# A new order of masks, projections and GpSimd work in a layer of attention and experts

## The reference

```python
qkv = jnp.einsum('bsm,qhdm->bqhsd', x, W_qkv)            # 16 heads of 64
qk_rot = qk * cos + _rotate_half(qk) * sin               # first 32 dims of q and k
scores = jnp.where(causal, -jnp.inf, Q @ K^T) / sqrt(DK)
out = softmax(scores) @ V ; attention = out @ W_o
probs = softmax(x @ router_w + router_b)                 # 8 experts and a skip
top_v, top_i = jax.lax.top_k(probs, 2)
experts = sum over the two of gate * (gelu(x @ w1[e]) @ w2[e]) + gate[skip] * x
```

## Time and profile before

| | |
|---|---|
| median of 3 runs | 1558.59 us |
| profiled execution | 1554.54 us, its span 1552.7 us |
| mean granted clock of TensorE | 0.947 of full |
| PE / DVE / ACT / POOL busy | 81% / 78% / 73% / 52% of the span |
| instructions | 47377 |

### The profile page before, as it was taken

The page is one execution under the profiler, slowest core; times in us unless marked ns, Lnnn a source line. Parts: engine busy times, 40 slices in busy tenths (PEclk is TensorE's granted clock), DMA queues, the critical chain, the costliest instruction groups (busy, mean ns, idle before and its releaser), DMA issues.

```text
span 1552.7 us, 47377 instructions
## 1 busy us (share of the span) xinstructions
PE 1263.4 (81%) x15156; PEld 982.4 (63%) x15157; DVE 1213.7 (78%) x4592; ACT 1134.4 (73%) x3606; POOL 806.5 (52%) x1324
## 2 busy tenths in 40 slices
PE   2415888888888888887899999788888888888887
PEld 2403666666666666665798988566666666666666
DVE  6788777777778777775677777788888888887885
ACT  6415777777777777776588887777877777777776
POOL 3243666666666666665000000466766766666665
PEclk9757999999999999999899999999999999999999
DMA  9522322222222222224122322333333333333330
GB/s 296 183 52 52 79 73 70 71 69 69 70 71 69 70 71 70 69 71 133 52 84 85 88 83 79 77 77 78 76 79 76 86 91 83 81 90 95 79 76 26
DMA packets 115839, 130.19 MB, mean 84 GB/s; under 512 B 11568, under 2 KB 75312, under 8 KB 115376
## 3 DMA queue, kind: packets, MB, share of 16 engines
q1 hardware_dynamic: 107056, 110.26, 28.2%
q0 software_dynamic: 8576, 17.33, 3.9%
HBM read 28.85 MB, written 31.59 MB: 39 GB/s over the span
## 4 chain that ended last, share of the span: by engine, by line
PE 42%; DVE 26%; issue 8%; DMA 5%; POOL 4%; ACT 2%; DVEq 0%; POOLq 0%; ACTq 0%
PE bank L1118 8%; DVE arena L972 8%; PE bank L1189 7%; PE bank L1119 7%; PE bank L1120 7%; DVE arena L934 5%; DMA stage<-sorted_y_dram,rows_at 4%; PE bank L1225 4%; PE bank L1199 4%; DVE arena L945 3%; DVE o_whole L1005 2%; DVE arena L933 2%; PE bank L1209 2%; PE bank L1226 1%; DVE stage L891 1%
## 5 line engine op out<-in xcount | busy, mean ns | idle before, releaser
L643 ACT ACTIVATE probs<-arena,neg_max 128x128 f32<-128x128 f32 (+1 forms) x1024 | 453.3, 446 | 109.6 <-DVE neg_max L972 102.5
L972 DVE CUSTOM_DVE_ANT_0 arena<-bank,causal 128x128 f32<-128x128 f32 (+1 forms) x1024 | 314.8, 344 | 2.7 <-PE bank L1189 2.7
L1189 PE MATMUL bank<-arena 64*128 64x128 f16 (+1 forms) x3072 | 179.4, 252 | 128.8 <-DVE neg_max L972 128.3
L501 POOL DMA_INDIRECT stage<-sorted_y_dram,rows_at x128 | 126.3, 986 | 260.9 <-DMA sorted_y_dram<-stage 238.4
L1199 PE MATMUL bank<-ident,probs 128*128 128x128 f32 x1536 | 241.9, 274 | 5.7 <-ACT probsT L626 5.5
L1189 PEld LDWEIGHTS bank<-arena 64*128 64x128 f16 x3072 | 102.9, 97 | 182.8 <-DVE neg_max L972 128.5
L1199 PEld LDWEIGHTS bank<-ident,probs 128*128 128x128 f32 x1536 | 183.2, 142 | 35.7 <-issue 6.4
L626 ACT ACTIVATE probsT<-bank 128x384 f32<-128x384 f32 x384 | 185.9, 484 | 19.3 <-PE bank L1199 19.2
L643 ACT ACTIVATION_READ_ACCUMULATOR probs<-arena,neg_max 128x1 f32 x1024 | 195.4, 191 | 0.0
L1225 PE MATMUL bank<-probsT,arena 128*64 128x256 f32 x1024 | 187.6, 425 | 0.9 <-ACT probsT L626 0.9
L1118 PE MATMUL bank<-xnT_lo,wqk_hi 128*128 128x256 f16 x512 | 143.4, 280 | 54.9 <-DVE arena L934 50.8
(11 more groups left out here) (155 smaller groups left out, 3430.0 us busy)
## 6 DMA issues: line engine op xcount, KB each, us to landing
arena<-arena SPq DMA_DIRECT2D x256, 256.0 KB, 4.7
arena<-sorted_x_dram SPq DMA_DIRECT2D x72, 128.0 KB, 2.1
sorted_y_dram<-stage SPq DMA_DIRECT2D x72, 128.0 KB, 1.8
sorted_x_dram<-arena SPq DMA_DIRECT2D x3, 2304.0 KB, 16.7
arena<-experts_dram SPq DMA_DIRECT2D x8, 512.0 KB, 5.1
out_dram<-acc SPq DMA_DIRECT2D x32, 128.0 KB
sorted_x_dram<-arena SPq DMA_DIRECT2D x1, 2368.0 KB, 16.2
sorted_x_dram<-stage,rows_at POOLq DMA_INDIRECT x128, 2.3
```

What stands on the lines that cost most here:

```text
L501: nc.gpsimd.indirect_dma_start(out=stage[:, k % BACKS, :], out_offset=None, in_=sorted_y[0:ROWS, :], in_offset=bass.IndirectOffsetOnAxis(a ...
L643: last = nc.scalar.activation(probs[:, s % 4, at:at + w], masked[:, s % 4, at:at + w], ACT.Exp, bias=neg_max[:, s % 4, t:t + 1], scale=-1. ...
L972: last = nc.vector.tensor_tensor_reduce(out=masked[:, s % 4, at:at + w], in0=SC[s % 2][:, at:at + w], in1=causal[:, at:at + w], scale=1.0, ...
L1189: last = mm(SC[h][:, at:at + w], q_stack[parity][rows, r, ql, u, qs], k_stack[parity][rows, r, kl, u, 0:w], start=(n == 0), stop=(n == 2))
```

## The change

1. `mask(b, s)` becomes `masks(b, s)` at even s: both heads of a pair are masked one after the other, then everything else of the two steps follows. A wait for the exps of three heads earlier is added, since the masks run further ahead in their four buffers.
2. The units are placed anew: nine in steps 0 to 11 and five in steps 10 to 15, no longer eight projections in steps 0 to 7. Three of the eight projections of sample b + 2 (plain 0, rotary 0, plain 1) are made in sample b, at steps 10, 12 and 14. Samples 0 and 16 have a denser list (`OPENERS`).
3. ACT's `rope_high` moves from lag 2 to lag 3. The low parts of rotary queries (j = 0 and 1) move from DVE (lag 3) to GpSimd (lag 4); those of keys stay.
4. The rows to send are normalised on GpSimd, just ahead of their send, and the slots are read in place, without `rows_at`. GpSimd's waits for indirect DMAs stand right before what needs them; `pause` is gone. One gather moves from step 9 to 10.
5. Inverses are taken for four heads at once, at steps 0, 4, 8 and 12, behind that step's evictions, scaling and unit work; the splits follow directly.
6. In DVE's order `o_scale` stands before the unit work.

```diff
-BESIDE = [
-    [("rest", 0)], [("rope", 0)], [("rest", 1)], [("rope", 1)],
-    [("rest", 2)], [("rope", 2)], [("rest", 3)], [("rope", 3)],
-    [("v_high", 0)], [], [("v_high", 1)], [("y", 0)],
-    [("y", 1)], [("v_low", 0)], [("v_low", 1)], [],
-]
+OPENERS = ((0, "rest", 0), (1, "rope", 0), (2, "rest", 1), (3, "rope", 1), (4, "rest", 2), (6, "rope", 2),
+           (7, "v_high", 0), (8, "rest", 3), (9, "v_high", 1), (10, "rope", 3))
+USUAL = ((0, "rope", 1), (2, "rest", 2), (4, "rope", 2), (5, "v_high", 0), (6, "rest", 3), (7, "v_high", 1),
+         (8, "rope", 3), (9, "y", 0), (11, "y", 1))
+AHEAD = ((10, "rest", 0), (12, "rope", 0), (14, "rest", 1))
+VALUES = ((13, "v_low", 0), (15, "v_low", 1))
-GATHER_AT = [1, 3, 5, 7, 9, 9, 11, 13]
+GATHER_AT = [1, 3, 5, 7, 9, 10, 11, 13]
...
 def o_split(J, j, parity):
     pool.wait_ge(o_scaled, J + 1)
-    nc.gpsimd.tensor_tensor(pause[:], half[:, 0:1], half[:, 0:1], ALU.add)
...
+def q_rope_low(j, m):
+    pool.wait_ge(rope_hi, ROPES * m + j + 1)
+    hi, lo = parts("rope", j)
+    nc.gpsimd.tensor_tensor(lo, roped[j % 2], hi, ALU.subtract).then_inc(q_rope_lo, 1)
+
+def normalise_row(b, i):
+    tile = PER * b + i
+    pool.wait_ge(sent, 16 * TOP * tile)
+    nc.gpsimd.tensor_scalar(stage[:, i, :], acc[:, tile, :], neg_mean[:, tile:tile + 1], rstd[:, tile:tile + 1],
+                            ALU.add, ALU.mult).then_inc(send_ready, 1)
...
+# GpSimd, step s: o_split; rope_add of the unit at s - 1; q_rope_low of the rotary unit at s - 4 (j < 2);
+# then normalise_row (even k) and send, or gather
...
-for kind, j, u, psum, n in beside(b, at, s - 2):
+for kind, j, of, u, psum in due(b, s, 3):
     if kind == "rope":
-        rope_high(j, b + 1)
+        rope_high(j, of)
...
+def masks(b, s):
+    dve.wait_ge(s_ready, 8 * b + s // 2 + 1)
+    if not (b == 0 and s < 4):
+        dve.wait_ge(exp_done, 16 * b + s - 2)
+    for i in range(2):
+        for t, (at, w) in enumerate(((0, P), (P, 2 * P))):
+            last = nc.vector.tensor_tensor_reduce(out=masked[:, (s + i) % 4, at:at + w], ...)
+        last.then_inc(s_masked, 1)
+
+def invert(N, n):
+    dve.wait_ge(exp_done, QUAD * N + QUAD)
+    nc.vector.reciprocal(inv, total[:, of, :]).then_inc(inv_done, 1)
+    if N >= 2:
+        dve.wait_ge(inv_turned, 2 * N - 2)
+    dve.wait_ge(inv_done, N + 1)
+    nc.vector.tensor_scalar(hi, inv, W_SCALE, None, ALU.mult).then_inc(inv_hi, 1)
+    dve.wait_ge(inv_hi, N + 1)
+    nc.vector.scalar_tensor_tensor(lo, inv, W_SCALE, hi, ALU.mult, ALU.subtract).then_inc(inv_ready, 1)
...
+def beside(b, s, at):       # DVE: t_evict, o_scale, turn / rest_low / y_add of the unit at s - 1,
+                            # invert at s % 4 == 0, rope_low of a key unit at s - 3, mix at s == 0, combine
+def sample(b, parity, at):
+    for s in range(0, H, 2):
+        masks(b, s)
+        beside(b, s, at)
+        beside(b, s + 1, at)
```

More of the change, by code:

```diff
@@ L505, in sample @@
+            pool.wait_ge(routed, 1)
+            pool.wait_ge(cleared, 16 * 5)
             def sample(b, parity, at):
                 for s in range(H):
[L507 to L520, removed]
                     if not (at in FILLS and s < SPLIT_LAG) and (s - SPLIT_LAG) % 2 == 1:
                         o_split(8 * b + (s - SPLIT_LAG - 1) // 2, (s - SPLIT_LAG) % H // 2, parity if s >= SPLIT_LAG else 1 - parity)
-                    for kind, j, u, psum, n in beside(b, at, s - 1):
+                    for kind, j, of, u, psum in due(b, s, 1):
@@ L524, in sample @@
                         if kind == "rope":
[L525 to L529, removed]
+                            rope_add(j, of)
+                    for kind, j, of, u, psum in due(b, s, 4):
+                        if kind == "rope" and j < 2:
+                            q_rope_low(j, of)
+                    if b < MID and s in SEND_AT:
+                        k = SEND_AT.index(s)
+                        if k % TOP == 0:
+                            normalise_row(b, k // TOP)
+                        send(b, k)
@@ L531, in rest_of @@
+                    if b >= MID and s in GATHER_AT:
+                        gather(b, GATHER_AT.index(s))
             def rest_of(b):
@@ L917, in mix @@
             def mix(b):
+                if b < MID:
+                    dve.wait_ge(send_ready, TPS * b + TPS)
                 for t in range(TPS):
@@ L962, in _ @@
             router_mix()
-            def mask(b, s, at_fill):
-                if s % 2 == 0:
-                    dve.wait_ge(s_ready, 8 * b + s // 2 + 1)
-                    if not (at_fill and s < INV_LAG):
-                        invert(8 * b + (s - INV_LAG) // 2, (s - INV_LAG) % H // 2)
-                for t, (at, w) in enumerate(((0, P), (P, 2 * P))):
-                    last = nc.vector.tensor_tensor_reduce(
-                        out=masked[:, s % 4, at:at + w], in0=SC[s % 2][:, at:at + w], in1=causal[:, at:at + w],
-                        scale=1.0, scalar=MASKED, op0=ALU.add, op1=ALU.min, accum_out=neg_max[:, s % 4, t:t + 1])
-                last.then_inc(s_masked, 1)
-                if s % 2 == 0 and not (at_fill and s < INV_LAG):
-                    split_inverse(8 * b + (s - INV_LAG) // 2, (s - INV_LAG) % H // 2)
@@ new lines, in beside @@
+            def beside(b, s, at):
+                G = 16 * b + s
+                if not (at in FILLS and s < OUT_LAG) and (s - OUT_LAG) % 4 == 0:
+                    t_evict(G - OUT_LAG, (s - OUT_LAG) % 4)
+                if not (at in FILLS and s < SCALE_LAG) and (s - SCALE_LAG) % 2 == 1:
+                    o_scale(8 * b + (s - SCALE_LAG - 1) // 2, (s - SCALE_LAG) % H // 2)
+                for kind, j, of, u, psum in due(b, s, 1):
+                    if kind == "rope":
+                        turn(j, u, psum, of)
+                    elif kind == "rest":
+                        rest_low(j, psum, of)
+                    elif kind == "y":
+                        y_add(of, j, u, psum, at in (FORMER, TURN))
+                if not (at in FILLS and s < QUAD) and s % QUAD == 0:
+                    invert(G // QUAD - 1, (s // QUAD - 1) % QUAD)
+                for kind, j, of, u, psum in due(b, s, 3):
+                    if kind == "rope" and j >= 2:
+                        rope_low(j, of)
+                if s == 0:
+                    if b >= MID:
+                        mix(b)
+                    elif b > 0:
+                        mix(b - 1)
+                if b >= MID and s in COMBINE_AT:
+                    combine(b, COMBINE_AT.index(s))
```

170 lines of the change are left out of this document (56 added, 114 removed).

## The result

The changed kernel takes 1569.24 us (median of 12 runs, 1562.15 to 1575.69) against 1559.32 us of the kernel before (12 runs, 1553.65 to 1567.07): ratio 1.0057, 95% interval 1.0032 to 1.0082. It is slower by 0.6%, where 1487 us, 4.6% faster, was forecast. The profiled execution is the slowest of its twelve, 1575.69 us with a span of 1574.0; that of before, 1554.54, is among the fastest, so 11 of the 21 us between the two profiles are chance of the pick, 0.4 us of each sample.

The account below looks back on a forecast made before the run. The order in which engines release each other was taken as the bound. Former samples falling from 37.8 to 32.5 us (-79) and latter ones' +6 gave 1481.5, plus 4.1 and 1.5: 1487 us, range 1428 to 1535.

Parts of the forecast that it names:

- The former samples' sum: Samples of the former half: GpSimd's 31.4 us plus 1.1 for sums late to ACT, taken as 32.5 us each.
- two steps of slack: GpSimd's queue: output splits behind waiting rows or issues are needed by ACT's copy only two heads later; no cost counted.
- The latter samples' loop: Latter samples: turn, rotary sum, gather, landing, combine bound the period; four loops of 20.4 us within 36.3.
- the rest of DVE's path: Latter samples, from each combine to the next turn's end: 3.7 us, four times 14.8, plus mix 0.5 and additions 0.6.
- DVE's wait for gathers: Sign for the forecast, latter stretch: this wait should rise from 49.4 us to 90 or more.
- rival (e): GpSimd's query low parts block DVE one for one: 2.6 us a sample, 78 on the forecast, 1565 us; chance 0.04.
- Masks first: Masking both heads first opens the mask loop; PE's mask waits, 4.0 us a former sample, should go nearly whole.
- Spreading: Fourteen units spread over the steps let a sample run at the busiest engine's sum; PE's about 31 us.
- (b): Both halves gain: ACT or PE sets the latter period at 33 us, total 1437 us; chance 0.22.
- (c): Spread pays half: former samples 35.0 us, about 1523 total; sign: DVE idle behind exps or ACT; chance 0.19.
- (d): GpSimd becomes the bound through longer low parts and rows: former samples 38.2 us, total 1611 us; chance 0.11.
- Slower: Outcome of a kernel slower than before, from most of the GpSimd-bound and DVE-blocking rivals; chance 0.12.

Follow-up runs that it names:

- x4: The changed kernel with each row normalised one send earlier; 1548.3 us, ratio 0.9915 to the kernel before.
- x2: The changed kernel with each row's second send going to a table of its own, the second choice left out of the result; 1540.3 us, ratio 0.9866.
- x5: The changed kernel with gather first in its GpSimd step, rows normalised one send earlier and query low parts back on DVE; 1497.4 us, ratio 0.9615.
- x6: The changed kernel with gather first in its GpSimd step and rows normalised one send earlier; 1474.0 us, ratio 0.9465.
- x10: x6 plus the two send tables of x2, the second choice left out of the result; 1473.5 us, ratio 0.9439.
- x11: x6 with DVE's key low parts one step later; 1481.9 us, ratio 0.9497.
- x13: x10 with GpSimd's query low parts one step later, second choice still left out; 1476.7 us, ratio 0.9473.
- x1: The changed kernel with the gather at the head of its GpSimd step, before output split and rotary sum; 1486.8 us, ratio 0.9542.
- x3: The changed kernel with the two query low parts moved back from GpSimd to DVE; 1530.4 us, ratio 0.9811.
- x7: The kernel before with only both masks of a pair first, including the wait for earlier exps; 1562.4 us, ratio 1.0032.
- x9: x6 with the projection units in the places of the kernel before; 1553.8 us, ratio 0.9962.

## Why the prediction was wrong

**The former samples' sum (32.5 us; measured 35.9, so 3.4 x 15 = 51 us).** The term that failed is GpSimd's: 31.4 us of instructions, with the waits of its sends for the landing of the send before put at nothing, covered by "two steps of slack". They measured 7.8 us a sample (80.6 + 21.3 in 13), and the trace of the kernel before already had as much (103.0 us at L487). The instructions were sized well: a query low part takes 1.17 us (1.27 taken), a row 0.45 (0.4), a send 1.02. But in steps 3, 7, 11 and 15 only an output split of 1.3 us lies between two sends; a landing of 2.3, and 4.2 beside stacks, doesn't fit. A queue that is 74% busy (148.88 of 200) held the others back, for it also stood still in order. x4 and x2 give back 1.6 and 1.9 us of the 3.4. The rest, 34.0 to 34.5 in seven versions with the new places (x2, x4, x5, x6, x10, x11, x13), stayed over the forecast with the landings or the key's wait taken away. PE is busy 373.6 of 400 us in x6, 32.0 us a sample where "about 31" was taken; 1.1 us above that would still be 1 us short. Which wait closes that gap is open.

**The latter samples' loop (36.3; measured 38.8, 2.5 x 15 = 37 us).** The loop was rightly named, and x1 shows it: it is what the change lost. Its sum was mis-sized. In the sample shown above the four loops take 22.0 us for the 20.4 of the forecast, the rest of DVE's path 16.9 for 15.9. The term that failed in the loops is the combine at 0.4 us: it takes 1.80 in the first, held by the gather's issue (1234.17) and the query low part (1235.17) that the change had put right behind it, and 1.07 in the fourth. Over 91 combines the mean is 0.58, for eight a sample 1.4 us over 0.4 each; with the query low parts off GpSimd (x3) the period is 37.2. In the rest of the path no run tells the terms apart, except that `mix` takes 0.88 us for 0.5. One sign did not come: DVE's wait for gathers should have risen from 49.4 us to 90 or more, and it is 46.5 (1000 to 1514 us):

```profile
DVE acc L888 <- DMA stage<-sorted_y_dram,slots: 46.5, 37, 2.6
```

In two loops of four DVE waits for ACT's high part in its stead (34.9 us in the same stretch), a wait that the forecast does not have; there the loops' times came out near the forecast (5.2 for 5.7, 4.9 for 5.0) by another path than the one foretold, which is luck. So rival (e)'s mechanism was real and stood on the bounding path, not as a cost of its own. Where the DVE low part of the earlier trace rows held GpSimd for 0.3 us, GpSimd here held DVE for 1.5. The Trainium skill (SBUF — State Buffer, "Who interferes with whom") states that a DVE instruction with two SBUF inputs, as the combine is, contends with a GpSimd instruction that reads SBUF, for one exclusive lock. The trace agrees, with the combine's end at 1236.5 behind the low part's at 1236.3. That section also has the order of issue decide who blocks; here the combine came second to the gather's issue but before the low part (1234.69 against 1235.17), and sat through both. Another share may be the clock: after such a stall PE works at its low level, as the row above shows; how much of the 2.5 us that is was not measured apart.

**Masks first.** The waits went as foretold (52.0 to 0.2 us), and the time did not: x7. A wait that two engines share in a loop was read as the price of the loop. The wait for the projection banks, 39.3 us in x7, had been there before with 19.7, right behind the masks.

**Spreading.** Right in its sign, and larger than the whole net forecast: x9 puts the new places at 80 us once GpSimd's order is mended. That the levelling of DVE and PE is the reason is argued, not shown.

**The rivals.** (b) was held too unlikely for its reason: the latter period of 33 is real, but only with the gather moved. (c) came nearest to the former period (35.0 for 35.9), and its sign came: DVE stands 57.7 + 42.9 us behind ACT at its low parts. But with the landings out of the way (x2) the same two waits are 34.3 + 16.2 us (176 to 640), so half of them came from GpSimd's queue, and taking the second away (x11) gains nothing. (d) named the right engine for the former samples for a wrong reason, the length of its instructions. Slower had 0.12. The fault of the sum was to add a gain of 79 us with an untested slack to a loss whose combine was counted at its undisturbed length.

## What to carry to other kernels

Before work is moved to an engine with time to spare, write out its queue in order with its DMA waits: a wait for a landing inside the queue costs that engine like an instruction, and 74% busy did not mean room for more. Where one engine starts a transfer that another consumes at a fixed step, look at what the issue stands behind: the instruction whose landing is awaited goes first in its step, which here was worth 5%, and mending the order around a change can be worth more than the change. A wait that vanishes is no gain until the next one in the same loop has been priced.

## What was not expected of the hardware

- A DVE instruction on 128 x 8 elements took 1.86 us when it met GpSimd's issue of an indirect DMA and a 512-column subtraction back to back; with that subtraction moved away (x13) its group's mean is 0.26.
- In the place shown above GpSimd starts the next send 0.77 us after the landing that it waits for (432.94 to 433.71; the chain of waits of the changed kernel; start, us, what):

```profile
428.73 4.21 DMA sorted_x_dram<-stage,slots
...
432.98 0.73 issue
433.71 1.02 POOL sorted_x_dram L493
```

- An indirect send of 64 KB (128 rows of 128 numbers of four bytes) landed in 2.3 us in the middle and in 6.2 at most; the late one shown above, 4.2, lay beside the stacks. Issue to landing of line 493, changed kernel:

```profile
DMA to landing us min/median/max: 2.3/2.3/6.2
```
